# A transformer layer on one core: the value bias moves from VectorE into TensorE's accumulation, ScalarE takes the values out, and the slots are set anew

## What is computed

```
xn   = layernorm(x)
q    = xn @ Wq.T + bq          v = xn @ Wv.T + bv        (16 heads of 8)
hash = 6 sign bits of (q, 1) @ hyperplanes, per head and row -> a bucket number
s    = q q^T / sqrt(128) * (62 + [same bucket])
x1   = x + layernorm(softmax(s) v)
out  = x1 + layernorm(ffn(layernorm(x1)))
ffn: silu(a w1) * (a w2), gelu(. h1), gelu(. h2), . w3    (128 -> 512 -> 512 -> 512 -> 128)
```

## Time and profile before

| | us |
|---|---|
| median of 3 runs (1383.75 to 1386.71) | 1386.21 |
| profiled execution, device time | 1381.73 |
| profiled execution, span of the profile | 1379.9 |
| busy: PE, DVE, POOL, ACT | 1241.7, 1233.4, 1221.8, 1066.0 |

### The profile page before, as it was taken

The page is one execution under the profiler, slowest core; times in us unless marked ns, Lnnn a source line. Parts: engine busy times, 40 slices in busy tenths (PEclk is TensorE's granted clock), DMA queues, the critical chain, the costliest instruction groups (busy, mean ns, idle before and its releaser), DMA issues. The chain is left out here.

```text
span 1379.9 us, 19626 instructions
## 1 busy us (share of the span) xinstructions
PE 1241.7 (90%) x5302; PEld 493.5 (36%) x5394; DVE 1233.4 (89%) x3965; ACT 1066.0 (77%) x1445; POOL 1221.8 (89%) x259
## 2 busy tenths in 40 slices
PE   3666899999999999999999999999999999998897
PEld 1111234333333434333343433333343333334343
DVE  4988999999999999999999999999999999999420
ACT  2354677979797887979798797979879797879852
POOL 2699989999999999999999999999999999999910
PEclk9876899999999999999999999999999999999999
DMA  3564445444543555454545544544454444444100
GB/s 105 148 187 112 129 113 151 120 130 126 132 137 118 133 136 138 105 145 120 133 116 143 131 126 123 135 128 131 119 154 119 120 130 124 138 121 106 54 5 11
DMA packets 89470, 167.37 MB, mean 121 GB/s; under 512 B 18192, under 2 KB 54160, under 8 KB 89360
## 3 DMA queue, kind: packets, MB, share of 16 engines
q1 hardware_dynamic: 89252, 165.82, 44.4%
q10 hardware_dynamic: 108, 0.30, 0.1%
HBM read 150.59 MB, written 15.47 MB: 120 GB/s over the span
## 5 line engine op out<-in xcount | busy, mean ns | idle before, releaser
L987 POOL TENSOR_TENSOR logits<-max_row,logits 128x4096 f32<-128x4096 f32 x128 | 1139.2, 8916 | 69.3 <-DMA max_row<-max_scratch 67.0
L810 DVE CUSTOM_DVE_ANT_0 logits<-s_bank,coeff 128x512 f32<-128x512 f32 x1024 | 690.2, 675 | 0.0
L1039 ACT ACTIVATE logits<-logits 128x1024 f32<-128x1024 f32 x512 | 507.8, 1047 | 52.1 <-POOL logits L987 50.9
L760 DVE TENSOR_SCALAR coeff<-brow,bcol 128x516 bf16<-128x516 bf16 x1024 | 482.1, 471 | 50.3 <-PE s_bank L552 36.7
L552 PE MATMUL s_bank<-mov_stack,stat_stack 128*128 128x512 bf16 x932 | 330.1, 394 | 49.9 <-DVE rowmax L810 41.6
L572 PE MATMUL aux_bank<-logits,v_pad 128*32 128x512 f32 x2048 | 268.7, 622 | 26.2 <-ACT logits L1039 16.2
L703 PE MATMUL f_bank<-hid_b,h_sb 128*128 128x512 f32 x512 | 250.7, 597 | 0.8 <-ACT hid_b L1154 0.6
L692 PE MATMUL f_bank<-hid_a,h_sb 128*128 128x512 f32 x512 | 243.8, 592 | 0.1
L552 PEld LDWEIGHTS s_bank<-mov_stack,stat_stack 128*128 128x128 bf16 x1024 | 98.0, 98 | 383.5 <-issue 195.4
L692 PEld LDWEIGHTS f_bank<-hid_a,h_sb 128*128 128x128 f32 x512 | 95.0, 190 | 86.5 <-issue 78.0
L703 PEld LDWEIGHTS f_bank<-hid_b,h_sb 128*128 128x128 f32 x512 | 93.8, 190 | 77.4 <-issue 66.5
(11 more groups left out here) (101 smaller groups left out, 912.6 us busy)
## 6 DMA issues: line engine op xcount, KB each, us to landing
max_row<-max_scratch SPq DMA_DIRECT2D x128, 512.0 KB, 4.2
brow<-bucket_scratch SPq DMA_DIRECT2D x63, 522.0 KB, 6.4
mov_stack<-q_scratch SPq DMA_DIRECT2D x192, 96.0 KB
stat_stack<-q_scratch SPq DMA_DIRECT2D x189, 96.0 KB
max_scratch<-rowmax_T SPq DMA_DIRECT2D x512, 1.0 KB
q_scratch<-q_parts SPq DMA_DIRECT2D x16, 384.0 KB, 4.7
x_in<-in_x SPq DMA_DIRECT2D x16, 256.0 KB, 3.1
q_scratch<-q_parts SPq DMA_DIRECT2D x16, 256.0 KB, 5.1
```

Of the source, the lines that this page charges most:

```text
L760: nc.vector.tensor_scalar(coeff[:, k % 3, :].rearrange("p (r n) -> p r n", r=ROW_RUNS), brow[:, h // 4 % 2, h % 4, :, 0:RUN], bcol[:, b % ...
L810: nc.vector.tensor_tensor_reduce(out=logits[:, ring(b, k), :], in0=tile_bank(k)[:], in1=coeff[:, k % 3, 0:SEQ], scale=float(E) ** -0.5, sc ...
L987: nc.gpsimd.tensor_tensor(tiles, max_row[:, m % 2].unsqueeze(2).broadcast_to([P, GROUP, ST, SEQ]), tiles, ALU.subtract).then_inc(below_max ...
L1039: nc.scalar.activation(logits[:, first:first + 2, :], logits[:, first:first + 2, :], ACT.Exp, scale=-1.0).then_inc(probs_done, 1)
```

## The change

The bias is split once, at the start, into three bf16 parts (high, middle, low), which lie in partitions 0 to 31, 32 to 63 and 64 to 127 of `v_bias`. `v_select` is a bf16 matrix with ones in rows 0, 32 and 64. One product of the two writes the bias into all 128x512 of the bank, and the four value products add to it. VectorE's add is gone; a plain copy on ScalarE, behind the exponential of slot 32, writes `v_pad`. The bias row is loaded into `ffn`, which is not in use yet. At the same time some forty slot constants are changed. The code:

```
...
+                    pe.wait_ge(v_select_made, 1 + PARTS)
+                    pe.wait_ge(v_bias_steps, 6)
+                    nc.tensor.matmul(projection_bank(p, 1)[:], v_select[:], v_bias[:], start=True, stop=False)
                     for t in range(ST):
                         last = nc.tensor.matmul(projection_bank(p, 1)[:, t * P:(t + 1) * P], xnT[:, t * P:(t + 1) * P], wv_sb[:],
-                                                start=True, stop=True)
+                                                start=False, stop=(t == ST - 1))
...
+            def split_value_bias():
+                nc.vector.memset(v_select[:], 0.0).then_inc(v_select_made, 1)
+                dve.wait_ge(v_select_made, 1)
+                for n in range(PARTS):
+                    nc.vector.memset(v_select[32 * n:32 * n + 1, :], 1.0).then_inc(v_select_made, 1)
+                nc.vector.tensor_copy(v_bias[:], bv_sb).then_inc(v_bias_steps, 1)
+                dve.wait_ge(v_bias_steps, 1)
+                nc.vector.tensor_tensor(bv_sb, bv_sb, v_bias[:], ALU.subtract).then_inc(v_bias_steps, 1)
+                dve.wait_ge(v_bias_steps, 2)
+                nc.vector.tensor_copy(v_bias[32:64, :], bv_sb[32:64, :]).then_inc(v_bias_steps, 1)
+                nc.vector.tensor_copy(v_bias[64:P, :], bv_sb[64:P, :]).then_inc(v_bias_steps, 1)
+                dve.wait_ge(v_bias_steps, 4)
+                nc.vector.tensor_tensor(bv_sb[64:P, :], bv_sb[64:P, :], v_bias[64:P, :], ALU.subtract).then_inc(v_bias_steps, 1)
+                dve.wait_ge(v_bias_steps, 5)
+                nc.vector.tensor_copy(v_bias[64:P, :], bv_sb[64:P, :]).then_inc(v_bias_steps, 1)
...
-                if k == V_ADD_SLOT:
-                    dve.wait_ge(v_psum, p + 1)
-                    nc.vector.tensor_tensor(v_pad..., projection_bank(p, 1)..., bv_sb..., ALU.add).then_inc(v_added, 1)
...
+                if k == V_COPY_SLOT:
+                    act.wait_ge(v_psum, p + 1)
+                    nc.scalar.copy(v_pad..., projection_bank(p, 1)...).then_inc(v_copied, 1)
```

The split stands in VectorE's stream ahead of the first query's remainder (L854). The slots that change an order in the steady iterations:

```
-FIRST_HIDDEN_SLOTS = (56, 56, 58, 61, 62, 62, 63, 64, 64, 67, 67, 72, 72, 73, 73, 75)
+FIRST_HIDDEN_SLOTS = (56, 56, 59, 61, 62, 62, 63, 64, 64, 65, 67, 73, 73, 73, 73, 74)
-SECOND_HIDDEN_SLOTS = (77, 80, 81, 83, 83, 83, 86, 88, 88, 88, 90, 91, 92, 95, 96, 98)
+SECOND_HIDDEN_SLOTS = (79, 79, 79, 81, 82, 82, 87, 88, 88, 88, 90, 90, 92, 93, 98, 99)
-OUTPUT_SLOTS = (100, 103, 105, 105)      GATE_SLOTS (.., 49)   MULTIPLY_SLOTS = (47, 48, 52, 52)
+OUTPUT_SLOTS = (101, 104, 105, 105)      GATE_SLOTS (.., 50)   MULTIPLY_SLOTS = (46, 46, 52, 52)
-X_STATS_SLOT = 2    XNT_SLOT = 58    Q_COPY, Q_HIGH = 56, 57    V_SLOT = 29    PROJ, BITS = 25
+X_STATS_SLOT = 4    XNT_SLOT = 57    Q_COPY, Q_HIGH = 58, 58    V_SLOT = 30    PROJ, BITS = 26
-ATT_NORM_SLOT = 29  RESIDUAL_SLOT = 32  Y1_MOMENTS = 34  END_STATS = 44  END_RSTD, END_NORM = 54, 54
+ATT_NORM_SLOT = 31  RESIDUAL_SLOT = 33  Y1_MOMENTS = 35  END_STATS = 46  END_RSTD, END_NORM = 57, 59
-STORE_SLOT = 1  X_LOAD_SLOT = 0  ROW_STORE_SLOT = 43  (X_RES_SLOT = 46 stays)
+STORE_SLOT = 4  X_LOAD_SLOT = 4  ROW_STORE_SLOT = 41
```

More of the change, by code:

```diff
@@ L56 @@
 EPS = 1e-5
-GATE_SLOTS = (44, 45, 48, 49)
+GATE_SLOTS = (44, 45, 48, 50)
 UP_SLOTS = (46, 47, 51, 52)
-FIRST_HIDDEN_SLOTS = (56, 56, 58, 61, 62, 62, 63, 64, 64, 67, 67, 72, 72, 73, 73, 75)
-SECOND_HIDDEN_SLOTS = (77, 80, 81, 83, 83, 83, 86, 88, 88, 88, 90, 91, 92, 95, 96, 98)
[L63 to L67, removed]
+FIRST_HIDDEN_SLOTS = (56, 56, 59, 61, 62, 62, 63, 64, 64, 65, 67, 73, 73, 73, 73, 74)
+SECOND_HIDDEN_SLOTS = (79, 79, 79, 81, 82, 82, 87, 88, 88, 88, 90, 90, 92, 93, 98, 99)
+SILU_SLOTS = (41, 48)
+MULTIPLY_SLOTS = (46, 46, 52, 52)
+OUTPUT_SLOTS = (101, 104, 105, 105)
+FIRST_GELU_SLOTS = (67, 70)
+SECOND_GELU_SLOTS = (86, 96)
 F_BANKS = 3
@@ L80 @@
 DIVIDE_LAGS = (39, 40)
[L84 to L89, removed]
+X_STATS_SLOT = 4
+LATE_X_STATS_SLOT = 33
+X_MOMENTS_SLOT = 21
+LATE_X_MOMENTS_SLOT = 34
+X_PREPARE_SLOT = 16
+LATE_X_PREPARE_SLOT = 35
 X_RSTD_SLOT = 35
-LATE_X_RSTD_SLOT = 45
-X_NORM_SLOT = 49
+LATE_X_RSTD_SLOT = 42
+X_NORM_SLOT = 50
 XNT_COPY_SLOT = 54
-XNT_SLOT = 58
-Q_COPY_SLOT = 56
+XNT_SLOT = 57
+Q_COPY_SLOT = 58
 Q_SLOT = 61
-Q_HIGH_SLOT = 57
-V_SLOT = 29
-V_ADD_SLOT = 32
+Q_HIGH_SLOT = 58
+V_SLOT = 30
+V_COPY_SLOT = 32
 Q_REST_SLOT = 61
-PROJ_SLOT = 25
-BITS_SLOT = 25
+PROJ_SLOT = 26
+BITS_SLOT = 26
 Q_MIDDLE_SLOT = 58
@@ L108 @@
 ROW_SLOT = 37
-ROW_COPY_SLOT = 34
+ROW_COPY_SLOT = 33
 ATT_STATS_SLOT = 24
 ATT_MOMENTS_SLOT = 26
-ATT_PREPARE_SLOT = 25
+ATT_PREPARE_SLOT = 27
 ATT_RSTD_SLOT = 31
-ATT_NORM_SLOT = 29
-RESIDUAL_SLOT = 32
+ATT_NORM_SLOT = 31
+RESIDUAL_SLOT = 33
 Y1_STATS_SLOT = 33
-Y1_MOMENTS_SLOT = 34
+Y1_MOMENTS_SLOT = 35
 Y1_PREPARE_SLOT = 36
-Y1_RSTD_SLOT = 39
+Y1_RSTD_SLOT = 36
 Y1_NORM_SLOT = 37
@@ L125 @@
 FFN_SLOT = 39
[L126 to L131, removed]
+END_STATS_SLOT = 46
+END_MOMENTS_SLOT = 52
+END_PREPARE_SLOT = 51
+END_RSTD_SLOT = 57
+END_NORM_SLOT = 59
+Y2_SLOT = 61
 SUB_SLOT = 9
@@ L139 @@
 GT = GROUP * ST
[L140 to L148, removed]
+STORE_SLOT = 4
+LOAD_SLOT = 5
+Q_STORE_SLOT = 35
+FIRST_XNT_SLOT = 13
+FIRST_Q_STORE_SLOT = 34
+X_LOAD_SLOT = 4
+ROW_STORE_SLOT = 41
+STACK_SLOT = 9
+FFN_LOAD_SLOT = 24
 FFN_LOAD_STEP = 3
@@ L242, in sandwich_kernel @@
         ffn = sb("ffn", [P, ST, E])
+        bv_sb = ffn[:].rearrange("p t e -> p (t e)")
         s_bank = [bank(f"s_bank{n}") for n in range(S_BANKS)]
@@ L265, in sandwich_kernel @@
         v_psum = sem("v_psum")
-        v_added = sem("v_added")
+        v_copied = sem("v_copied")
+        v_select_made = sem("v_select_made")
+        v_bias_steps = sem("v_bias_steps")
         proj_psum = sem("proj_psum")
@@ L848, in query_step @@
                 if k == Q_REST_SLOT:
+                    if not begun(p):
+                        dve.wait_ge(projection_in, 16 * PROJECTION_DMAS)
+                        split_value_bias()
                     dve.wait_ge(q_part_steps, 4 * p + 1)
                     dve.wait_ge(q_done, p + 1)
-                    if not begun(p):
-                        dve.wait_ge(projection_in, 16 * PROJECTION_DMAS)
                     nc.vector.scalar_tensor_tensor(out=aux_bank[:], in0=aux_bank[:], scalar=bq_sb[:],
@@ L1087, in project_step @@
             def project_step(p, k):
+                if k == V_COPY_SLOT:
+                    act.wait_ge(v_psum, p + 1)
+                    if p > 1:
+                        act.wait_ge(pv_psum, (p - 1) * QUADS)
+                    if p == 0:
+                        act.wait_ge(v_pad_clear, 2)
+                    nc.scalar.copy(
+                        v_pad[:, p % 2, :, 0:PAD_PITCH - HALF_W].rearrange("p r (h w) -> p r h w", w=VW)[:, :, :, 0:DH],
+                        projection_bank(p, 1)[:].rearrange("p (r h d) -> p r h d", r=2 * ST, d=DH)).then_inc(v_copied, 1)
                 if k == BCOL_COPY_SLOT:
```

19 lines of the change are left out of this document (5 added, 14 removed).

## The result

The changed kernel takes 1392.49 us (median of 5, 1391.16 to 1397.98) where the kernel before takes 1386.21 (median of 5): ratio 1.0056, 95% interval 1.0039 to 1.0073. It is slower by 6.3 us; the forecast was 1381.5, faster. The profiled execution took 1397.98, span 1396.2, and is the longest of the five: its 16.3 us over the span before overstate the loss, but it shows the places.

The account below looks back on a forecast made before the run. A closed path through group 1's subtraction, exponentials, weighing and FFN takes 79.31 us a round. Thirteen rounds at -0.35, +0.45 at the start and -0.6 in batch 0 give -4.7: 1386.21 to 1381.5, range 1371 to 1390.

Parts of the forecast that it names:

- The two rings: Two nearly equally long closed paths, one through GpSimd's subtraction and ScalarE's exponentials, one of TensorE and VectorE alone.
- the copy: ScalarE's copy into v_pad, between group 1's last exponential and the weighing: +0.59 us a round in the first ring.
- the output slots: OUTPUT_SLOTS 100 to 101 puts eight products behind the row product; TensorE's idle before the transpose goes: -0.91 a round.
- the first ring: Group 1's transpose, subtraction, exponentials, weighing, transpose L645, next round's transpose: 79.31 us, forecast to change by -0.32 a round.
- The query's slots: QHIGH comes forward, the end's scaling goes behind; VectorE's 0.27 wait before L854 goes: 0 to -0.27 a round.
- The load of x: SP issues x just before the load of group 7's maxima: +0.25 us a round, bounds 0 and 1.1.
- The hidden slots: Hidden layers' products spread otherwise; VectorE's idle 0.89 goes, with the add shortening the second ring by 1.5 or more.
- The bias product: TensorE's bf16 product at slot 30: about 0.3, at most 0.59, counted 0 as covered by idle before the weighing.
- Batch 0: VectorE runs there without a gap, so the add's absence counts whole: -0.6 us.
- The start: Bias split hidden in VectorE's idle stretch; one more bf16 product at lower clock delays the first scores: +0.45 us.
- signs of being right: Weighing released by the copy, transpose 9.4 after it, VectorE's idle 0.89 and 0.27 gone, period 78.9 to 79.1.
- the slower rival: Load of x holds up groups 7 and 0's maxima on SP: +0.5 a round, 1393 us; 20 in a hundred.

Follow-up runs that it names:

- e10: Kernel before with the bias by TensorE's product and ScalarE's copy, plus OUTPUT_SLOTS as in the change: 1376.61 us, ratio to before 0.9928.
- e1: Kernel before with only the bias by TensorE's product and ScalarE's copy, every slot as before: 1388.29 us, ratio to before 1.0019.
- e12: e4 with ScalarE's copy done twice, the first into a tile nobody reads: 1383.28 us, ratio to before 0.9984.
- e9: Kernel before with OUTPUT_SLOTS alone as in the change, VectorE's add kept: 1383.43 us, ratio to before 0.9976.
- e15: e9 with VectorE's multiply moved earlier (MULTIPLY_SLOTS as in the change), add kept: 1381.68 us, ratio to before 0.9971.
- e4: Changed kernel with the end's scaling back at slot 54 and the load of x back at slot 0: 1376.76 us, ratio to before 0.9930.
- e5: Kernel before with the end's reciprocal and scaling late, behind the query's copies on ScalarE: 1397.01 us, ratio to before 1.0096.
- e3: Changed kernel with only the load of x back at the head of SP's order: 1389.77 us, ratio to before 1.0030.
- e6: Kernel before with x loaded late, between the store and load of group 7's maxima: 1394.3 us, ratio to before 1.0071.
- e2: Changed kernel with only the end's reciprocal and scaling back at slot 54: 1387.08 us, ratio to before 0.9997.
- e11: e9 with the hidden layers' slots as in the change, VectorE's add kept: 1392.01 us, ratio to before 1.0029.
- e7: All slots of e4, but VectorE's add in place of product and copy: 1377.58 us, ratio to before 0.9946.
- e14: e4 with the load of x moved behind the load of group 7's maxima: 1390.82 us, ratio to before 1.0036.

## Why the prediction was wrong

*The two rings, the copy, the output slots: right.* The copy costs 0.40 in unhindered rounds (14.90 for 14.50) and 0.42 to 0.59 in the mean (e10, e1); the forecast was +0.59. It lies in the first ring (e12). Weighing to transpose gives -0.99 (forecast -0.91). The add's absence gives nothing alone and the output slot little alone; together -10 us (e10, e9, e1, e15). The sum for the first ring, -0.32, was -0.58. With no cost for x the prediction's -0.5 a round would have given 1386.21 - 13 x 0.5 - 0.15 = 1379.6; e4, which has x where it was before, took 1376.76.

*The query's slots, "the end's scaling behind them": the step that failed.* The prediction took this move as something that only brings QHIGH forward, 0 to -0.27, and its front said of GpSimd that its order stays. The order does stay, but a wait in it grew: in place of a gain of 0 to 0.27, GpSimd waits 2.6 us a round. The scaling was never followed to its reader, GpSimd's add L1017, ahead of the subtraction of group 6, nor the add to its own reader, SP's store of the output, ahead of x and of group 7's maxima. The move costs 12 to 13 us alone (e5, and e3 against e4), with what it does to x included.

*The load of x: right mechanism, wrong size.* Forecast +0.25 a round with bounds 0 and 1.1, because "between the store's issue and the load the queue moves nearly nothing". Alone it costs 9.5 to 10.3 us (e6, e2 against e4), 0.75 a round. What was missed is the next group: x delays the load of group 0's maxima, which waits for their store (4.42 from store to load in e6, 3.26 before), as well as the landing of group 7's. The rival that named it got 20 in a hundred and gave 1393, which is near the measured time by luck: it had half of the reason, and the move that it left out is the larger one.

*The hidden slots* shorten tiles 10 to 24 as forecast (14.76 in unhindered rounds of e4, 15.56 before); 0.25 comes back between 24 and 36 (1.0 in e11), which the prediction didn't count. *The bias product* takes 0.40, not 0.3 (6.0 us in 15, by the groups of the changed kernel). *Batch 0* ends at 101.90, before at 102.07, with a first tile that is later by 0.52, so batch 0 itself is 0.69 shorter: in this trace the forecast of -0.6 is there. In other traces without the add batch 0 ends at 104.15 (e1) and 102.47 (e4), so it is not seen there.

*The start:* the first tile comes at 29.88 instead of 29.36, +0.52 for +0.45. The first bias product takes 0.59, as forecast (0.60); the prediction put that length down to a lower clock, but the granted clock in the profile reads 1.00 from 20 to 30 us, so this trace doesn't show the reason. The split itself is hidden: it ends at 14.3 and VectorE then still waits 1.42 before L879. Its second cast is worth a look. VectorE, and GpSimd at the same time:

```profile
8.65 3.96 DVE L802 CAST v_bias<-ffn 32x512 bf16<-32x512 f32 x1
12.64 0.52 DVE L803 CAST v_bias<-ffn 64x512 bf16<-64x512 f32 x1
```

```profile
8.61 3.72 POOL L1026 MEMSET v_pad<- 128x4352 f32 x1
```

A cast that takes 0.42 to 0.52 elsewhere in the split took 3.96 and ended 0.28 after GpSimd's memset did. By the Trainium skill (SBUF — State Buffer, "Who interferes with whom") a VectorE copy or cast in a two-port mode and a GpSimd instruction lock each other out for a whole instruction; this trace agrees (3.96 beside 3.72), and the split ended about 3.5 later for it, with no loss.

*The signs.* Of the prediction's signs of being right, most came: the copy holds the weighing in 14 rounds, TensorE's 0.91 ahead of the transpose is down to 0.14 or nothing, the transpose comes 9.33 behind the weighing, VectorE's 0.27 is gone and its 0.89 is 0.23. The one that sums them up did not: the period is 80.42, not 78.9 to 79.1, and two tiles ahead of that 0.89 VectorE now waits 1.94 in the mean where it waited 0.48. Of its signs of being wrong one came: VectorE's statistics of x (L819, now L843) wait for the load of x 11 times, 4.7 us in all, where they never did before; that is the slower rival's sign. The other sign of that rival misled: the waits for max_row fell to 51.2 instead of rising above 67, while the maxima came later, for the wait was booked on the add ahead.

What stays open: whether V_SLOT alone explains e11's extra 1.0 between tiles 24 and 36; how the changed kernel's loss is to be split between the two moves, since they overlap (16 to 17 us together, 23.3 as a sum); how much of the late scaling's 12 to 13 us is GpSimd's wait and how much the x that it makes late, which a kernel with a late scaling and the output's store out of SP's way would show; and why the add costs 7 us beside the output slot alone (e9, e10) and next to nothing with all of e4's slots (e7).

## What to carry to other kernels

When a step is moved on one engine, look up who reads its result and what stands behind that reader in the reader's own in-order stream; then do the same for the reader's result. Here one add held a subtraction on GpSimd and a load on SP. A small instruction without a deadline (1.3 us here) is as dangerous as a large one if something with a deadline (8.9 us, no slack) is queued behind it. Where two rings are nearly equal, judge edits to either only together: here +3 us and -3 us alone made -10 us.

## What the hardware showed that was not expected

A load of 256 KB issued within the 10 us between one group's store and the next group's load cost some 0.75 us a round ahead of the 512 KB load of that stretch (e6, and e2 against e4) and 1.1 behind it (e14 against e4, by the ratios); issued 4 to 5 us earlier, in the pause ahead of group 7's store, it left the chain alone (e4). And the shortest round comes back to the hundredth in kernels with different orders and the same VectorE work: 78.94 in the kernel before, 78.95 in e9, 78.92 in e15. It is no constant of that work, though: e7 does the same on VectorE and has 78.50.
